# One core, a four-layer transformer kernel: the tail of expert routing in another form

## The chip, the cores and the metric

The kernel runs on one core of a Trainium2 chip, as one program. The metric is the device time of one execution in microseconds (us), the median of several. Engines are TensorE (PE in the rows), VectorE (DVE), ScalarE (ACT), GpSimd (POOL), and SyncE (SP), which issues most DMA transfers.

## The reference

Eight batches of 100 tokens of width 512 pass through four residual layers: an alignment with a context of 722 rows by dynamic time warping, a mixture of 16 experts of which each token takes 3, latent attention, and a second mixture. The change touches the second layer, on its side that decides which expert gets which token:

```
raw_gate = softmax(einsum('btd,de->bte', x, gate))          # 8 x 100 x 16
_, topk_idx = top_k(raw_gate, 3)
mask = one_hot(topk_idx, 16).sum(axis=2)
gate_topk = mask * raw_gate
gate_topk = gate_topk / maximum(sum(abs(gate_topk), -1), 1e-12)
hidden = relu(einsum('btd,edh->bteh', x, W1) + b1)
out = einsum('bte,bted->btd', gate_topk, einsum('bteh,ehd->bted', hidden, W2) + b2)
```

Here x is already the layer-normalised output of the first layer.

## The kernel before

The program is a row of stages, `distances`, `warp`, `route`, `experts`, `attend_full`, `attend`, `feed_forward`. Each is a block with one instruction stream for each engine. A stage frees its semaphores and passes a barrier of all engines before the next begins. Inside a stage the order on an engine is the order of the code, and semaphores are the only ties between engines. `link` (a helper) makes each VectorE instruction wait for the one before.

`route` has two parts. In **the path stream**, for each batch b, TensorE multiplies the path with the context rows (`along_path`, L1025), VectorE adds the product to x (L1101), widens the next path and takes layer norm statistics (L1105 to L1110), TensorE transposes the result (`turn`, L1033), VectorE copies that to SBUF (`keep_T`, L1097), and TensorE makes the 16 logits of each token (`logits`, L1041), all in one PSUM tile `pl`. SP meanwhile stores x and the normalised rows to DRAM.

In **the tail** everything is done for all 8 batches at once. VectorE takes the softmax (with an exponential on ScalarE), `max` and `max_index` per batch, one-hot masks `hot`, their sum `chosen` (L1134), and the gates. TensorE counts ranks with two f32 products (L1056, L1057). VectorE adds totals over batches one by one, counts the tiles of 128 slots that each expert needs, and gets the slot of every (token, choice) pair. Slots are then inverted into tables by slot: VectorE compares each slot with 35 tile starts (`over`, L1163) and makes `in_tile` (the place inside a tile, 24 x 128 elements, L1169), GpSimd makes `of_tile` with three channels (1, token, gate; L1002 to L1006), and 24 f32 products on TensorE sum `in_tile` against `of_tile` (L1065). VectorE reads off the indices `gidx`, `oidx` and the gates `gate_s` (L1172 to L1175), and GpSimd gathers the first three tiles of rows (L1012). The loop `keep_awake` (L81) fills TensorE with f32 products of the identity whose results nobody reads: 36 before the inversion, 40 after it. Each f32 product is two rows (passes) in the trace.

`experts` starts with two transposes of gathered tiles (L1257). Then it runs 27 tiles of 128 slots, each with 32 + 8 f32 products; the third gathered tile is first used in the middle of the first of them.

Of the kernel before, what the change touches and what calls it, by code (L numbers as in the profile page):

```python
# [15 lines left out]
P = 128  # L16
# [20 lines left out]
NG = 3  # L37
# [863 lines left out]
def route(nc, io, res):  # L901

    ctx = ExitStack()
    with ctx:
# [9 lines left out]
        logit = sb("logit", [S, B, E_N])  # L914
        prob = sb("prob", [S, B, E_N])
        lmax, lsum = sb("lmax", [S, B]), sb("lsum", [S, B])
        top = sb("top", [S, B, 8])
        topi = sb("topi", [S, B, 8], U32)
        topf = sb("topf", [S, B, 8])
        tsum = sb("tsum", [S, B])  # L920
        iota_e = sb("iota_e", [S, E_N])
        hot = [sb(f"hot{k}", [S, B, E_N]) for k in range(TOPK)]
        chosen = sb("chosen", [S, B, E_N])
        before = sb("before", [S, S])
        tot = sb("tot", [S, B, E_N])
        off = sb("off", [S, B + 1, E_N])
        ntile, tiles_to, one_e = sb("ntile", [S, E_N]), sb("tiles_to", [S, E_N]), sb("one_e", [S, E_N])
        slot = sb("slot", [S, B, E_N])
        picked = sb("picked", [S, B, E_N])
        slotf = sb("slotf", [S, TOPK, B])  # L930

        KB, NT = TOPK * B, SLOT_TILES
        in_tile = res["reach_mem"][0:S, 0:KB * P].rearrange("p (i j) -> p i j", j=P)
        spare = ctx_rows[0:S, :, :].rearrange("p t d -> p (t d)")
        over = spare[:, 0:KB * (NT + 1)].rearrange("p (i t) -> p i t", t=NT + 1)
        of_tile = spare[:, KB * (NT + 1):KB * (4 * NT + 1)].rearrange("p (i c t) -> p i c t", c=3, t=NT)
        tile0, slot0, token = sb("tile0", [S, NT + 1]), sb("slot0", [S, P]), sb("token", [S, TOPK, B])
        tnum, within, dump = sb("tnum", [S, KB]), sb("within", [S, KB]), sb("dump", [P, 2])
        where_to = sb("where_to", [P, NT])
        ptab = pb("ptab", [P, 3 * NT])  # L940
        over_ok, tile_ok, of_ok, in_ok, tab_mm, idx_ok, kept_rows = (sem(n) for n in (
            "over_ok", "tile_ok", "of_ok", "in_ok", "tab_mm", "idx_ok", "kept_rows"))
# [3 lines left out]
        pl = pb("pl", [S, B, E_N])  # L946
        prank = pb("prank", [S, B * E_N])
        ptot = pb("ptot", [S, B, E_N])
        path_in, gate_in = res["path_in"], sem("gate_in")
        pathf_ok, px_ok, x_ok, var_ok, st_ok, xn_ok = (sem(n) for n in ("pathf_ok", "px_ok", "x_ok", "var_c", "st_c", "xn_ok"))  # L950
        pt_ok, xnT_ok, pl_ok, sub_ok, exp_ok, cs_ok = (sem(n) for n in ("pt_ok", "xnT_ok", "pl_ok", "sub_ok", "exp_ok", "cs_ok"))
        cs0, hot_ok, rank_ok = (sem(n) for n in ("cs0", "hot_ok", "rank_ok"))
# [27 lines left out]
        def _(pool):  # L980
            pool.iota(iota_e[:, :], pattern=[[1, E_N]], base=0, channel_multiplier=0,
                      allow_small_or_imprecise_dtypes=True).then_inc(cs_ok, 1)
            pool.memset(before[:, :], 1.0).then_inc(cs0, 1)
            pool.wait_ge(cs0, 1)

            pool.affine_select(out=before[:, :], in_=before[:, :], compare_op=ALU.is_gt, fill=0.0, base=0,
                               pattern=[[1, S]], channel_multiplier=-1).then_inc(cs_ok, 1)
            pool.iota(tile0[:, :], pattern=[[P, NT + 1]], base=0, channel_multiplier=0,
# [3 lines left out]
            pool.iota(token[:, :, :], pattern=[[0, TOPK], [S, B]], base=0, channel_multiplier=1,  # L992
                      allow_small_or_imprecise_dtypes=True).then_inc(cs_ok, 1)
            pool.iota(dump[:, 0:1], pattern=[[0, 1]], base=XT, channel_multiplier=1,
                      allow_small_or_imprecise_dtypes=True).then_inc(cs_ok, 1)
            pool.iota(dump[:, 1:2], pattern=[[0, 1]], base=-XT, channel_multiplier=-1,
# [3 lines left out]
            pool.wait_ge(cs_ok, 8)  # L1000
            pool.wait_ge(over_ok, 1)
            pool.tensor_tensor(of_tile[:, :, 0, :], over[:, :, 0:NT], over[:, :, 1:NT + 1], ALU.subtract).then_inc(tile_ok, 1)  # L1002
            pool.wait_ge(tile_ok, 1)
            pool.tensor_tensor(of_tile[:, :, 1, :], of_tile[:, :, 0, :],
                               token[:, :, :].rearrange("p k b -> p (k b)").unsqueeze(2).broadcast_to([S, KB, NT]), ALU.mult).then_inc(of_ok, 1)
            pool.tensor_tensor(of_tile[:, :, 2, :], of_tile[:, :, 0, :],  # L1006
                               res["gates"][:, :, :].rearrange("p k b -> p (k b)").unsqueeze(2).broadcast_to([S, KB, NT]), ALU.mult).then_inc(of_ok, 1)

            pool.wait_ge(idx_ok, 1)
            pool.wait_ge(kept_rows, 32 * B)  # L1010
            for i in range(NG):
# [1539 lines left out]
```

## Time and profile before

| what | value |
|---|---|
| median of 3 runs | 1208.29 us (1207.68 to 1208.56) |
| the profiled execution, its own time | 1209.34 us |
| its span, first to last instruction | 1207.7 us |
| mean granted TensorE clock | 0.95 of full |
| TensorE busy | 1074.1 us (89%) |
| VectorE busy | 460.0 us (38%) |
| ScalarE busy | 336.7 us (28%) |
| GpSimd busy | 224.6 us (19%) |

The share of an engine is an average over the stages; what a change in `route` is worth is read inside that stage. `route` runs from 274.7 us to about 379 us of the span, `experts` from there to about 800 us. Starts in the rows are us from the start of the span.

### The profile page before, as it was taken

The numbers are of one execution on the slowest core, as the hardware profiler recorded it, in microseconds if no ns is written. First come the engines' busy times: TensorE is split into PE (matmuls) and PEld (weight loads), VectorE is DVE, ScalarE is ACT, GpSimd is POOL, SyncE is SP. The second block draws the span as 40 slices with busy tenths as digits, with TensorE's granted clock in tenths as the row PEclk, the third lists the DMA queues.
The fourth block names the chain that finished last, engine by engine and source line by source line (L and its number), as shares of the span: only waits on it lengthen the run. The fifth ranks groups of instructions, "written<-read, shape, count | busy, mean of one in ns | idle before, by whom it ended". The sixth has DMA issues, their size and how long they took to land. (4 is left out here: it accounts for less than half of the span.)

```text
span 1207.7 us, 17529 instructions
## 1 busy us (share of the span) xinstructions
PE 1074.1 (89%) x5498; PEld 702.9 (58%) x5499; DVE 460.0 (38%) x1698; ACT 336.7 (28%) x802; POOL 224.6 (19%) x341
## 2 busy tenths in 40 slices
PE   8966679937949999999999999949999999999997
PEld 8952235524448777677766777635446665555554
DVE  7847888883570000000000010036765463121212
ACT  4424756770001222222222222214245430000000
POOL 0963021110021121121111111210030001121211
PEclk9978799968969999999999999969999999999999
DMA  8876005128404575856596555560021005000000
GB/s 302 227 169 219 1 1 183 53 99 220 152 14 164 156 246 183 283 193 218 182 311 201 182 182 183 173 196 10 0 77 64 1 1 157 1 1 1 14 14 28
DMA packets 71763, 152.84 MB, mean 127 GB/s; under 512 B 12026, under 2 KB 16258, under 8 KB 70870
## 3 DMA queue, kind: packets, MB, share of 16 engines
q1 hardware_dynamic: 63454, 131.21, 32.0%
q0 software_dynamic: 6928, 17.04, 6.3%
q10 hardware_dynamic: 1320, 3.84, 1.2%
q8 instruction: 30, 0.49, 0.2%
q14 instruction: 31, 0.25, 0.1%
HBM read 131.83 MB, written 20.25 MB: 126 GB/s over the span
## 5 line engine op out<-in xcount | busy, mean ns | idle before, releaser
L1305 ACT ACTIVATE att<-phid,b 128x128 f32<-128x128 f32 x216 | 79.3, 367 | 306.8 <-PE phid L1274 306.8
L1327 DVE TENSOR_TENSOR att<-py,att 128x512 f32<-128x512 f32 x27 | 18.7, 692 | 367.3 <-PE py L1282 367.3
L1274 PEld LDWEIGHTS phid<-tiles,shared 128*128 128x128 f32 x896 | 111.5, 192 | 37.4 <-issue 37.4
L1274 PEld LDWEIGHTS phid<-tiles,Wmem 128*128 128x128 f32 x832 | 103.5, 192 | 39.1 <-issue 39.1
L1274 PE MATMUL phid<-tiles,shared 128*128 x896 | 114.4, 276 | 1.2 <-issue 0.5
L1274 PE MATMUL phid<-tiles,Wmem 128*128 x832 | 106.3, 276 | 5.8 <-issue 4.5
L1282 PE MATMUL py<-shared,att 128*128 128x512 f32 x224 | 110.0, 593 | 0.0
L1282 PE MATMUL py<-Wmem,att 128*128 128x512 f32 x208 | 102.3, 594 | 0.4 <-DMA att<-in_b 0.4
L2365 PE MATMUL acc<-tiles 128*128 128x400 f32 x256 | 90.6, 505 | 0.0
L2431 DVE SCALAR_TENSOR_TENSOR tiles<-bf,shared 128x400 f32<-128x400 f32 x64 | 32.4, 567 | 130.3 <-PE bf L2350 129.6
L2324 PE MATMUL bf<-shared,Wmem 128*128 128x400 f32 x192 | 70.0, 501 | 2.0 <-PEq L49 1.3
L2365 PEld LDWEIGHTS acc<-tiles 128*128 128x128 f32 x256 | 47.1, 190 | 40.4 <-issue 8.6
L1349 POOL DMA_INDIRECT sum_d<-att,to_row x27 | 43.0, 1594 | 144.4 <-DVE att L1330 144.4
L2274 POOL TENSOR_TENSOR tiles<-tiles 128x400 f32<-128x400 f32 x32 | 32.4, 1033 | 153.8 <-DVE tiles L2431 153.8
L2324 PEld LDWEIGHTS bf<-shared,Wmem 128*128 128x128 f32 x192 | 36.1, 190 | 29.9 <-issue 2.0
L887 DVE TENSOR_TENSOR_SCAN cost_mem<-reach_mem,cost_mem,enter 128x93 bf16<-128x93 bf16 x115 | 47.2, 411 | 11.8
L1770 DVE RECIPROCAL shared<-shared 128x400 f32<-128x400 f32 x16 | 42.4, 2652 | 21.0 <-ACT shared L1677 20.7
L2291 ACT COPY outT<-acc 128x400 f32<-128x400 f32 x4 | 1.8, 495 | 172.4 <-PE acc L2365 172.4
L81 PE MATMUL px<-ident 128*128 128x128 f32 x188 | 27.2, 317 | 24.0 <-DMA path<-ctx_rows 16.3
L1492 PE MATMUL ba<-shared,Wmem 128*128 128x400 f32 x128 | 46.1, 504 | 2.6 <-DVE qT L1773 1.5
L1282 PEld LDWEIGHTS py<-shared,att 128*128 128x128 f32 x224 | 36.1, 192 | 13.4 <-issue 13.4
L209 POOL TENSOR_SCALAR Wmem<-slots_row,pos_k 128x128 bf16<-128x128 f32 x48 | 39.9, 850 | 20.6 <-DVE pos_k L143 20.6
(388 smaller groups left out, 1715.5 us busy)
## 6 DMA issues: line engine op xcount, KB each, us to landing
Wmem<-in_W SPq DMA_DIRECT2D x16, 2048.0 KB, 14.2
shared<-in_W SPq DMA_DIRECT2D x16, 2048.0 KB, 11.9
cT<-in_ctxT SPq DMA_DIRECT2D x8, 1444.0 KB, 11.8
ctx_rows<-in_ctx SPq DMA_DIRECT2D x8, 1280.0 KB
Wmem<-in_Wkv SPq DMA_DIRECT2D x2, 2048.0 KB, 9.2
att<-in_b SPq DMA_DIRECT2D x16, 256.0 KB, 14.3
tiles<-in_WoT SPq DMA_DIRECT2D x4, 1024.0 KB
Wmem<-in_WiT SPq DMA_DIRECT2D x3, 1024.0 KB, 7.1
```

Source lines behind the costliest of these rows:

```text
L209: pool.tensor_scalar(sel[:, b, t, :], slots_row[:, :], pos[:, t, b:b + 1], None, ALU.is_equal)
L887: dve.tensor_tensor_scan(walk[:, q, 1:NO], code[:, q, :], enter[:, :], walk[:, q, 0:1], ALU.mult, ALU.max).then_inc(scanned_r, 1)
L1274: ins = pe.matmul(ph[j % NH][:, :], W1[u][:, k, j * P:(j + 1) * P], xgT[:, bass.ds(w, 1), k * P:(k + 1) * P].rearrange("p o t -> p (o t)") ...
L1282: ins = pe.matmul(py[:, :], hT[:, j - 2, :], W2[u][:, j - 2, :], start=j == 2, stop=j == HJ + 1)
L1305: act.activation(hT[:, j, :], ph[j % NH][:, :], ACT.Relu, bias=b1[:, bass.ds((e + u) * HJ + j, 1)]).then_inc(relu_ok, 1)
L1349: pool.indirect_dma_start(out=res["sum_d"], out_offset=bass.IndirectOffsetOnAxis(ap=to_row[:, 0:1], axis=0), in_=y[:, :], in_offset=None, ...
L1492: ins = pe.matmul(qk_b[j % 3][:, 0:NH2], w, lnT[:, k, g * NH2:(g + 1) * NH2], start=k == 0, stop=k == KD - 1)
L1770: link(dve.reciprocal(inv[j % 2][:, :], inv[j % 2][:, :]))
L2274: pool.tensor_tensor(hs[i % 4][:, :], h1[i % 4][:, :], h2[i % 2][:, :], ALU.add).then_inc(hs_ok, 1)
L2324: pe.matmul(bank[i % NBK][:, 0:NT4], Wi[k][:, f * P:(f + 1) * P], xT[:, k, g * NT4:(g + 1) * NT4], start=k == 0, stop=False)
L2365: ins = pe.matmul(acc[k][:, 0:NT4], WoT[:, f, k * P:(k + 1) * P], hs[i % 4][:, :], start=f == 0, stop=f == FJ - 1)
L2431: dve.scalar_tensor_tensor((h1[i % 4], h2[i % 2])[k][:, :], bank[i % NBK][:, 0:NT4], 0.0, wb[k][:, g * NT4:(g + 1) * NT4], ALU.max, ALU.mu ...
```

## The change

It rewrites the tail and moves part of it:

- **Three best per batch, in the stream.** `best(b)` takes `max` and `max_index` straight from the PSUM logits (two banks in turn, so TensorE now waits on `pl_rd`), makes `hot` for the three choices and `chosen`, in bf16. `below_best(b)` subtracts the largest logit. Both are done for batch b-2 in iteration b; the last two batches follow after the last `keep_T`. No softmax is needed to choose.
- **Ranks.** A scan along batches (`upto`) replaces the additions per batch; three bf16 products give totals and ranks. Tiles of an expert come from one comparison, one reduction and one scan.
- **Slots inverted by codes.** The tile number is the slot as an integer, shifted right by 7. `same` (24 x 34) marks the tile, `of_tile` has two bf16 channels (batch code by VectorE, row code by ScalarE), `in_tile` is bf16, and 24 bf16 products yield one code from which both indices are made. GpSimd does nothing in between.
- **Gates last.** Softmax sums and gates come after the indices, split into three bf16 parts, and have 24 bf16 products of their own.
- **Gathers.** Two in `route`, the third at the head of GpSimd's part of `experts`.
- **`keep_awake`.** 8 before the last `turn`, 7 after the logits, 10 after the ranks, 10 after the indices' products and 16 after the gates' products, in place of 36 and 40.

The core of the diff:

```diff
+            def best(b):
+                dve.wait_ge(pl_ok, b + 1)
+                link(dve.max(top[:, b, :], pl[b % 2]))
+                dve.max_index(topi[:, b, :], top[:, b, :], pl[b % 2]).then_inc(pl_rd, 1)
+                dve.wait_ge(pl_rd, 2 * b + 1)
+                link(dve.tensor_tensor(hot[:, :, b, :], iota_e[...], topi[:, b, 0:TOPK][...], ALU.is_equal))
+                link(dve.tensor_tensor(chosen[:, :, b], hot[:, 0, b, :], hot[:, 1, b, :], ALU.add))
+                link(dve.tensor_tensor(chosen[:, :, b], chosen[:, :, b], hot[:, 2, b, :], ALU.add))
+            def below_best(b):
+                dve.tensor_scalar(logit[:, b, 0:E_N], pl[b % 2], top[:, b, 0:1], None, ALU.subtract).then_inc(pl_rd, 1)
...
                 if b:
                     keep_T(b - 1)
+                if b >= 2:
+                    best(b - 2)
+                    below_best(b - 2)
             keep_T(B - 1)
-            dve.wait_ge(pl_ok, B)
-            link(dve.tensor_reduce(lmax[:, :], pl[:, :, :], AX, ALU.max))
...
+            best(B - 2)
+            below_best(B - 2)
+            best(B - 1)
+            dve.tensor_tensor_scan(upto[...], fresh[...], chosen[...], 0.0, ALU.mult, ALU.add).then_inc(hot_ok, 1)
+            below_best(B - 1)
...
+            link(dve.tensor_copy(sloti[:, :], slotf[:, :]))
+            link(dve.tensor_scalar(tnum[:, :], sloti[:, :], 7, None, ALU.logical_shift_right))
+            dve.scalar_tensor_tensor(within[:, :], tnum[:, :], -float(P), slotf[:, :], ALU.mult, ALU.add)
+            dve.tensor_tensor(same, tile0[...], tnum[...], ALU.is_equal).then_inc(same_ok, 1)
+            dve.wait_ge(same_ok, 1)
+            dve.tensor_tensor(of_tile[:, :, 0, :], same, batch1[...], ALU.mult).then_inc(batch_ok, 1)
...
@@ TensorE
+                if n == B:
+                    pe.wait_ge(x_ok, B - 1)
+                    keep_awake(pe, px_whole[0], ident, 8)
...
-            keep_awake(pe, px_whole[0], ident, 36)
-            pe.wait_ge(of_ok, 2)
+            keep_awake(pe, px_whole[1], ident, 10)
+            pe.wait_ge(batch_ok, 1)
+            pe.wait_ge(row_ok, 1)
...
             ins.then_inc(tab_mm, 1)
-            keep_awake(pe, px_whole[0], ident, 40)
+            keep_awake(pe, px_whole[1], ident, 10)
+            for i in range(KB):
+                if i % B == 0:
+                    pe.wait_ge(gate_ok, i // B + 1)
+                ins = pe.matmul(pgate, in_tile[:, i, :], of_gate[:, i, :, :]..., start=i == 0, stop=i == KB - 1)
+            ins.then_inc(gate_mm, 1)
+            keep_awake(pe, px_whole[1], ident, 16)
```

**VectorE, end of the path stream, before.** From the normalisation of the last batch (`cost_mem<-x_res`) on; `xg_sb` holds the transposed rows, `pl` the logits.

```order
L1110 TENSOR_SCALAR cost_mem<-x_res,mv_c,rstd_c 100x512
L1097 COPY xg_sb<-pt 128x400 x2
L1115 TENSOR_REDUCE lmax<-pl 100x8
L1116 TENSOR_TENSOR logit<-pl,lmax 100x128
L1118 TENSOR_REDUCE lsum<-prob 100x8
```

The same place in the change:

```order
L1140 TENSOR_SCALAR cost_mem<-x_res,mv_c,rstd_c 100x512
L1113 COPY xg_sb<-pt 128x400
L1117 MAX top<-pl 100x8
L1118 MAX_INDEX topi<-top,pl 100x8
L1120 TENSOR_TENSOR hot<-iota_e,topi 100x3x16
L1122 TENSOR_TENSOR chosen<-hot 100x16
L1123 TENSOR_TENSOR chosen<-chosen,hot 100x16
L1126 TENSOR_SCALAR logit<-pl,top 100x16
L1113 COPY xg_sb<-pt 128x400
L1117 MAX top<-pl 100x8
```

The two copies of transposed rows stood side by side; now the six instructions for batch 5 stand between them, and those for batches 6 and 7 behind them.

**TensorE, from the last transposes to the end of `route`, before.** `px<-ident` is `keep_awake`.

```order
L1033 MATMUL pt<-ident,cost_mem 128x100 x4
L1041 MATMUL pl<-gate_w,xg_sb 100x16 x8
L1056 MATMUL prank<-chosen,before 100x128
L1057 MATMUL ptot<-chosen,ones 100x128
L81 MATMUL px<-ident 128x128 x36
L1065 MATMUL ptab<-ctx_rows,reach_mem 128x102 x24
L81 MATMUL px<-ident 128x128 x40
```

The same place in the change:

```order
L81 MATMUL px<-ident 128x128 x8
L1032 MATMUL pt<-ident,cost_mem 128x100 x4
L1042 MATMUL pl<-gate_w,xg_sb 100x16 x8
L81 MATMUL px<-ident 128x128 x7
L1062 MATMUL pt<-upto,all_rows 100x16
L1063 MATMUL prank<-chosen,before 100x128
L1064 MATMUL prank<-upto,all_rows 100x128
L81 MATMUL px<-ident 128x128 x10
L1071 MATMUL ptab<-ctx_rows,reach_mem 128x68 x24
L81 MATMUL px<-ident 128x128 x10
L1077 MATMUL px<-ctx_rows,reach_mem 128x102 x24
L81 MATMUL px<-ident 128x128 x16
```

Two long loops of fillers became five short ones, and a second set of 24 products, for the gates, stands behind the first.

## Rows read from the trace of the kernel before

**Rows 1.** Timeline of TensorE: start, length, instruction, count, [idle before, releaser].

```profile
332.10 0.80 PE L1041 MATMUL pl<-gate_w,xg_sb 128*100 128x16 f32 x8
...
343.87 0.75 PE L1056 MATMUL prank<-chosen,before 100*100 100x128 f32 x2 [5.58 <-DVE chosen L1134]
...
352.76 11.15 PE L81 MATMUL px<-ident 128*128 128x128 f32 x72 [7.71 <-DVE ctx_rows L1163]
363.75 5.50 PE L1065 MATMUL ptab<-ctx_rows,reach_mem 100*128 100x102 f32 x48
369.08 9.12 PE L81 MATMUL px<-ident 128*128 128x128 f32 x80
379.13 1.07 PE L1257 MATMUL ptx<-ident,xg_sb 128*128 128x128 f32 x8 [0.93 <-PEq L49]
...
389.33 0.60 PE L1257 MATMUL ptx<-ident,xg_sb 128*128 128x128 f32 x4
```

**Rows 2.** Stretches: us, busy (count) by engine, granted clock, DMA share, GB/s.

```profile
331.80:335.00 3.20, 1.25 (x14) 1.16 (x13) 2.63 (x7) 1.17 (x2) 0.00 (x0) 0.98 0.00 0
335.00:338.30 3.30, 3.29 (x20) 3.18 (x20) 0.85 (x2) 0.32 (x1) 0.00 (x0) 0.50 0.41 124
338.30:352.70 14.40, 1.17 (x4) 0.83 (x4) 12.21 (x72) 0.31 (x1) 0.00 (x0) 0.50 0.00 1
352.70:358.80 6.10, 6.04 (x28) 6.07 (x29) 6.03 (x5) 0.00 (x0) 5.95 (x3) 0.50 0.00 1
...
369.20:378.20 9.00, 9.00 (x81) 8.81 (x79) 0.71 (x4) 0.00 (x0) 3.02 (x3) 1.00 0.28 87
378.20:381.60 3.40, 1.11 (x10) 0.90 (x9) 1.42 (x2) 1.38 (x3) 0.00 (x0) 1.00 0.29 60
```

**Rows 3.** Timeline of VectorE, end of the path stream.

```profile
331.96 0.69 DVE L1101 TENSOR_TENSOR x_res<-x_res,px 100x512 f32<-100x512 f32 x1 [2.88 <-PE px L1025]
...
334.71 0.57 DVE L1097 COPY xg_sb<-pt 128x400 f32<-128x400 f32 x1
335.80 0.58 DVE L1097 COPY xg_sb<-pt 128x400 f32<-128x400 f32 x1 [0.52 <-PE pt L1033]
```

**Rows 4.** Timeline of VectorE, the tail.

```profile
340.20 0.71 DVE L1122 MAX8 top<-prob 100x8 f32<-100x16 f32 x8
...
341.03 0.17 DVE L1125 FIND_INDEX8 topi<-top,prob 100x8 uint32<-100x16 f32 x1
...
343.53 0.29 DVE L1134 TENSOR_TENSOR chosen<-chosen,hot 100x128 f32<-100x128 f32 x1
...
343.94 0.17 DVE L1138 TENSOR_SCALAR tsum<-tsum 100x8 f32<-100x8 f32 x1
...
351.58 1.03 DVE L1163 TENSOR_TENSOR ctx_rows<-slotf,tile 100x840 f32<-100x840 f32 x1
...
354.39 6.22 DVE L1169 TENSOR_TENSOR reach_mem<-slot,within 100x1024 f32<-100x1024 f32 x3
```

**Rows 5.** One line, L1169: count, ns min/median/max, first and last start.

```profile
L1169 DVE TENSOR_TENSOR reach_mem<-slot,within x3: 1224/2579/2579, 354.4 to 358.0; 100x1024 f32<-100x1024 f32 x3
```

**Rows 6.** Timeline of GpSimd, the tail.

```profile
357.00 2.54 POOL L1006 TENSOR_TENSOR ctx_rows<-ctx_rows,gates 100x816 f32<-100x816 f32 x1
370.32 1.11 POOL L1012 DMA_INDIRECT xg_sb<-xn_d,gidx  x1 [10.79 <-DVE gate_s L1175]
```

**Rows 7.** Groups of the page, the scan of `warp`: busy us, mean ns, idle before.

```profile
L887 DVE TENSOR_TENSOR_SCAN cost_mem<-reach_mem,cost_mem,enter 128x93 bf16<-128x93 bf16 x115 | 47.2, 411 | 11.8
```

**Rows 8.** Timeline of TensorE, bf16 products of `warp`.

```profile
85.58 0.80 PE L538 MATMUL pfil<-Wmem,onesw 128*128 128x128 bf16 x6
86.18 0.34 PE L536 MATMUL pidx<-where,Wmem 128*128 128x2 bf16 x6
86.39 0.80 PE L538 MATMUL pfil<-Wmem,onesw 128*128 128x128 bf16 x6
```

**Rows 9.** One line of ScalarE, L514: ns min/median/max.

```profile
L514 ACT ACTIVATE reach_mem<-rank_w,one x11: 772/829/836, 101.1 to 180.2; 128x460 bf16<-128x460 bf16 x10, 128x414 bf16<-128x414 bf16 x1
```

**Rows 10.** One line, L1343, the gathers in `experts`, issue to landing.

```profile
DMA to landing us min/median/max: 3.3/4.5/6.4
```

More of the change, by code:

```diff
@@ L923, in route @@
[L923 to L930, printed above, removed]
-        KB, NT = TOPK * B, SLOT_TILES
-        in_tile = res["reach_mem"][0:S, 0:KB * P].rearrange("p (i j) -> p i j", j=P)
@@ L934, in route @@
[L934 to L940, printed above, removed]
@@ new lines, in route @@
+        hot = sb("hot", [S, TOPK, B, E_N], BF16)
+        chosen, upto, fresh = (sb(n, [S, E_N, B], BF16) for n in ("chosen", "upto", "fresh"))
+        before, all_rows = sb("before", [S, S], BF16), sb("all_rows", [S, S], BF16)
+        limits, beyond = sb("limits", [S, MORE_TILES]), sb("beyond", [S, E_N, MORE_TILES])
+        ntile, tiles_to, one_e = sb("ntile", [S, E_N]), sb("tiles_to", [S, E_N + 1]), sb("one_e", [S, E_N])
+        slot, picked = sb("slot", [S, B, E_N]), sb("picked", [S, TOPK, B * E_N])
@@ new lines, in route @@
+        KB, NT = TOPK * B, SLOT_TILES
+        slotf = sb("slotf", [S, KB])
+        sloti, tnum = sb("sloti", [S, KB], I32), sb("tnum", [S, KB], I32)
+        within = sb("within", [S, KB], BF16)
+        in_tile = res["reach_mem"][0:S, 0:KB * P // 2].bitcast(BF16).rearrange("p (i j) -> p i j", j=P)
+        spare = ctx_rows[0:S, :, :].rearrange("p t d -> p (t d)")[:, 0:3 * KB * NT].bitcast(BF16)
+        same = spare[:, 0:KB * NT].rearrange("p (i t) -> p i t", t=NT)
+        of_tile = spare[:, KB * NT:3 * KB * NT].rearrange("p (i c t) -> p i c t", c=2, t=NT)
@@ new lines, in route @@
+        of_gate = spare[:, 3 * KB * NT:6 * KB * NT].rearrange("p (i c t) -> p i c t", c=3, t=NT)
+        tile0, slot0 = sb("tile0", [S, NT], BF16), sb("slot0", [S, P], BF16)
+        batch1, row1, dump = sb("batch1", [S, KB], BF16), sb("row1", [S, 1]), sb("dump", [P, 1])
+        gpart = sb("gpart", [S, KB, 3], BF16)
+        grest = sb("grest", [S, KB])
+        code, where_to = sb("code", [P, NT]), sb("where_to", [P, NT])
+        ptab = pb("ptab", [P, 2 * NT])
+        same_ok, batch_ok, row_ok, in_ok, gate_ok, tab_mm, gate_mm, idx_ok, kept_rows, pl_rd = (sem(n) for n in (
+            "same_ok", "batch_ok", "row_ok", "in_ok", "gate_ok", "tab_mm", "gate_mm", "idx_ok", "kept_rows", "pl_rd"))
@@ L1077, in _ @@
             act.activation(prob[:, :, :], logit[:, :, :], ACT.Exp).then_inc(exp_ok, 1)
+            act.wait_ge(cs_ok, NCONST)
+            act.wait_ge(same_ok, 1)
+            act.activation(of_tile[:, :, 1, :], same, ACT.Copy, scale=row1[:, 0:1]).then_inc(row_ok, 1)
         @block.vector
@@ L1170, in _ @@
                                   within[:, k * B:(k + 1) * B].unsqueeze(2).broadcast_to([S, B, P]), ALU.is_equal).then_inc(in_ok, 1)
+            dve.tensor_copy(res["table"][:, 0:E_N + 1], tiles_to[:, :])
             dve.wait_ge(tab_mm, 1)
-            dve.tensor_copy(res["gidx"][:, 0:NT], ptab[:, NT:2 * NT])
-            link(dve.tensor_scalar(where_to[:, :], ptab[:, 0:NT], dump[:, 1:2], dump[:, 0:1], ALU.mult, ALU.add))
-            dve.tensor_tensor(res["oidx"][:, 0:NT], where_to[:, :], ptab[:, NT:2 * NT], ALU.add)
@@ L1178 @@
+            for k in range(TOPK):
+                n = slice(k * B, (k + 1) * B)
+                dve.tensor_tensor(of_gate[:, n, :, :], same[:, n, :].unsqueeze(2).broadcast_to([S, B, 3, NT]),
+                                  gpart[:, n, :].unsqueeze(3).broadcast_to([S, B, 3, NT]), ALU.mult).then_inc(gate_ok, 1)
+            dve.wait_ge(gate_mm, 1)
+            dve.tensor_reduce(res["gate_s"][:, 0:NT], pgate.rearrange("p (c t) -> p t c", t=NT), AX, ALU.add)
 INNER, HEADS, DH = 512, 8, 64
```

159 lines of the change are left out of this document (74 added, 85 removed).

## The prediction

> **What bounds the kernel now.** I read the stage boundaries first, on TensorE's timeline. The path stream ends with the logits of batch 7 (338.30), the first product of `experts` starts at 379.13 [rows 1, 2], and in the 41 us between TensorE does nothing that anyone reads except two short rank products and the 48 passes of L1065. So `route`'s tail is a pure latency chain, and every us cut from it moves the whole rest of the program forward: `experts` starts with a barrier, and its loads of the second expert's weights are issued behind that barrier too, so they move along. Second I asked who holds the chain at each point:
>
> - 338.30 to 352.70: VectorE. Busy 12.21 of 14.40 us with 72 instructions, most with about 0.17 us of fixed cost [rows 2, 4].
> - 352.76 to 363.75: TensorE's own 72 filler passes, at half clock for the first 6 us, 28 rows in 6.10 us, 0.218 us each [rows 1, 2]. VectorE's `in_tile` ends at 360.61, GpSimd's last channel at 359.54 [rows 4, 6]; the fillers last longer and hold the 48 passes back by 3.1 us.
> - 369.08 to 378.20: 80 more filler passes at full clock, 81 rows in 9.00 us, 0.111 us each. Indices are ready and the gathers begin at 370.32 [rows 1, 2, 6]; nothing but these fillers holds the barrier, and TensorE's next product stands 0.93 us behind them [rows 1].
>
> The end of `route` is therefore set by TensorE's last filler, and I follow the chain to that point in both kernels.
>
> **The change, step by step.** Unit prices: 128 elements on VectorE 0.29 us, 840 elements 1.03 us [rows 4], so 0.16 us plus 1.04 ns per element; an instruction of 8 to 24 elements 0.17 to 0.20; a gap of 0.035 us between linked instructions.
>
> 1. *Stream.* `best` is MAX8 (0.16 alone; eight side by side took 0.71), the index search (0.17 and its load, 0.25 together), 48 elements (0.21), twice 16 elements (0.34), and `below_best` 0.17: with five gaps 1.3 us per batch [rows 4]. VectorE idles 2.88 us per batch waiting for L1025 [rows 3], and TensorE needs its result only after the next six long products. So batches 0 to 4 cost nothing. If that cover were gone it would be 1.3 us for each of 5 batches. Batch 5's six instructions stand ahead of the last `keep_T`: that copy started at 335.80, and now starts at 335.28 + 1.3 = 336.6 and ends at 337.2 [rows 3]. Logits of batch 7 are then 0.80 us, if the clock is full [rows 1], to 338.0. VectorE's work for batch 6 ends at 338.5, batch 7's at 339.65. The scan over 128 elements is unseen at that size; 93 took 0.41 [rows 7], so between 0.41 and 0.57, and I take 0.55. `chosen` and `upto` are there at **340.2**; before it was 343.82 [rows 4].
> 2. *Ranks.* TensorE has 7 fillers (14 passes) to finish first: 338.0 + 14 x 0.111 = 339.6 at full clock, + 14 x 0.218 = 341.1 at half. The first rows show the clock at half from 335.0 after only about 2 us of idling between the last context product and the last transposes [rows 2]; now 8 fillers stand there, but TensorE idles again from about 335.9 to 337.2. I take the low clock, hence 341.1, and 0.25 for the totals: **341.35**.
> 3. *Slots.* 96 elements twice (0.52), a scan of 16 (0.19), 128 elements (0.29), 384 twice (1.12), three of 24 (0.54), `same` 816 (1.01), nine gaps (0.33): 4.0 us, to **345.35**. Before, the same stretch ran from 345.1 to 352.6, over three times as many instructions.
> 4. *Inversion.* VectorE: one batch channel 1.05, `in_tile` 3 x 1.22, to **350.1**. The 1.22 is the fastest of the three before; the other two took 2.58 each while GpSimd's multiplications ran beside them [rows 5, 6], and GpSimd is silent now. ScalarE's channel: 460 elements took 0.83 [rows 9], so 816 take at most 1.47, done at 346.9, before the first third of `in_tile` (347.6). The last 8 of 24 bf16 products: twelve took 0.81 [rows 8], so 0.55, and 0.15 to land: **350.8**. Before it was 369.25.
> 5. *Indices and gates.* Reduction and `gidx` 0.5 (the two gathers follow, 2.5 us, covered), `where_to` and `oidx` 0.45, eleven small gate instructions with gaps 2.55, `of_gate` 3 x 1.03: 357.4. Ten fillers (2.2 to 4.4 us) lie in TensorE's wait for it. Last 8 products 0.7: **358.1**. All of this is new behind the index table: before, the gates cost 0.7 us ahead of it plus one GpSimd channel.
> 6. *Last fillers.* 16, so 32 passes x 0.111 = 3.55 at full clock, to **361.65**.
>
> Sum: 378.20 - 361.65 = 16.5 us. By parts: fillers at the end, 9.1 down to 3.55, give 5.6; the gate chain takes 7.3 back; the rest, 18.2, is the chain to the index table (369.25 to 350.8, less rounding). The extra constants on GpSimd lie in front of the stream, where VectorE waits anyway.
>
> The third gather now goes out behind the barrier, at about 0.5 to 1 us into `experts`, and is issued in 1.1 us. It is used 10.2 us after the stage's first product (389.33 against 379.13) [rows 1], and gathers there land in 3.3 to 6.4 us amid the weight loads [rows 10]: covered by about 2 us; if not, at most a few us once.
>
> *A rule weighed.* The bf16 operands could make the wide VectorE comparisons faster than the f32 rows. All rows of two-operand instructions of this width are f32 [rows 4, 5], so the trace does not show bf16: at an unchanged rate 1.22 us, at double rate 0.16 + 0.53 = 0.69 us. I take the f32 row. The Trainium skill, "VectorE: DVE Perf Modes" (the perf-mode tier table), says that a `tensor_tensor` on bf16 in SBUF runs at twice the f32 rate. "Vector Engine (DVE) Microarchitecture Reference" (Performance modes) adds that an operand which repeats one element ran at the single rate; that is the layout of `in_tile`, `of_tile` and `of_gate`. No run here shows either yet.
>
> **Rivals.**
>
> - *Forecast, 0.60:* as summed. The profiled execution would be 1209.34 - 16.5 = 1192.8; the median shown lies 1.05 us under the profiled time, so 1208.3 - 16.5 = 1191.8; I say **1192**. Its own range is 1190 to 1194, for the sizes of unseen instructions (about 1 us each way) and the 7 fillers (0.9).
> - *Low clock at the end, 0.22:* between the rank products and the index products VectorE keeps TensorE waiting over 5 us, of which 10 fillers cover 2.2 to 4.4, and the gate products come in three bursts. For it: about 2 us of idling sufficed before [rows 2]. Against it: the clock came back after 6.1 us of dense passes, even at half clock [rows 2], and index products plus 10 fillers are about that long. The last 32 passes then take 7.0 instead of 3.55: 1195.3. If `experts` also starts low, its first products pay up to 3 us more: 1198.
> - *Double rate, 0.08:* one `of_tile` channel saves 0.42, `in_tile` 3 x 0.53, `of_gate` 3 x 0.42: 3.3 us, 1188.7.
> - *Third gather late, 0.05:* it queues behind 4 MB of weights that SP issues in the same us and lands after them, some 3 to 4 us after its use: 1195.5.
> - *Slower, 0.02:* VectorE's added work in the stream doesn't fit. Its result feeds back to TensorE over `pl_rd`, in lock step. The cover is 2.88 us per batch; to lose the 16.5 us over six iterations it must overrun by 2.75 each, so cost 5.6 us instead of 1.3, 0.9 us per instruction. An instruction of 24 elements did take 0.67 beside GpSimd's work, but GpSimd has none in the stream. At 1.1 us each, it would be 1208.3 - 16.5 + 6 x 3.7 = 1214.
> - *Nothing gained, 0.03:* a wait that I don't see at the stage's end, such as for the gathers or stores, keeps the barrier near 378. Against it: gathers begin at 370.32 before and the stores were out long ago.
>
> **Numbers.** 1192. The range reaches from the double rate to the low clock at the end with part of a cold start: 1188.5 to 1197.5; less than 2 in 10 lies outside. What a measurement of this kernel can tell from no change is 0.2%, 2.4 us. Faster 0.95, same 0.02, slower 0.03 (part of the last two).
>
> **What would show it.** In the profile of the change: `upto` written near 340; `same` near 345.5; three L1174 instructions of 1.2 us each with nothing on GpSimd beside them; the first gather near 351.5; the last filler near 361.7 and the first product of `experts` 0.93 behind; `experts` and all later stages as long as before. L1131 must keep its 6.2 us rhythm. I would be wrong if that rhythm stretches, if the last 32 fillers last 7 us, if L1174 takes 0.7, or if TensorE waits for L1363's gather in the first tile.

## The result and the profile after

| | before | after |
|---|---|---|
| median of 4 runs, us | 1207.99 (1207.40 to 1208.56) | 1192.56 (1192.04 to 1194.04) |
| the profiled execution, own time | 1209.34 | 1192.04 |
| its span | 1207.7 | 1190.4 |
| mean granted TensorE clock | 0.950 | 0.958 |

The ratio after / before is 0.9874 [0.9857, 0.9891]: 15.4 us less.

Busy times of the profiled execution after, first page:

```profile
PE 1064.0 (89%) x5447; PEld 694.0 (58%) x5448; DVE 464.1 (39%) x1711; ACT 338.1 (28%) x803; POOL 218.8 (18%) x342
```

TensorE has 10 us less of busy time than before and VectorE 4 us more. These sums say nothing of the order of the work; the tail's timeline does. TensorE after, in the columns of [rows 1]:

```profile
336.75 3.33 PE L81 MATMUL px<-ident 128*128 128x128 f32 x14
339.88 0.22 PE L1062 MATMUL pt<-upto,all_rows 100*100 100x16 bf16 x1
...
340.18 3.66 PE L81 MATMUL px<-ident 128*128 128x128 f32 x20
...
348.57 0.63 PE L1071 MATMUL ptab<-ctx_rows,reach_mem 100*128 100x68 bf16 x8 [0.50 <-DVE reach_mem L1174]
349.01 4.34 PE L81 MATMUL px<-ident 128*128 128x128 f32 x20
...
355.53 0.55 PE L1077 MATMUL px<-ctx_rows,reach_mem 100*128 100x102 bf16 x8 [0.37 <-DVE ctx_rows L1200]
355.92 3.80 PE L81 MATMUL px<-ident 128*128 128x128 f32 x32
360.66 1.06 PE L1285 MATMUL ptx<-ident,xg_sb 128*128 128x128 f32 x8 [0.94 <-PEq L49]
363.16 4.56 PE L1302 MATMUL phid<-tiles,Wmem 128*128 x24 [1.44 <-ACT att L1326]
367.55 1.02 PE L1310 MATMUL py<-Wmem,att 128*128 128x512 f32 x2
```

The first product of `experts` starts at 360.66 where it started at 379.13 [rows 1]. That is 18.5 us, but not all of it is the change's: the tail itself began earlier in this trace. VectorE after:

```profile
324.06 0.69 DVE L1131 TENSOR_TENSOR x_res<-x_res,px 100x512 f32<-100x512 f32 x1 [1.15 <-PE px L1024]
...
330.27 0.69 DVE L1131 TENSOR_TENSOR x_res<-x_res,px 100x512 f32<-100x512 f32 x1 [1.47 <-PE px L1024]
...
338.22 0.42 DVE L1150 TENSOR_TENSOR_SCAN upto<-fresh,chosen 100x128 bf16<-100x128 bf16 x1
340.14 0.26 DVE L1156 TENSOR_TENSOR beyond<-pt,limits 100x96 f32<-100x96 f32 x1 [1.27 <-PE pt L1062]
...
343.06 1.00 DVE L1169 TENSOR_TENSOR ctx_rows<-tile,tnum 100x816 bf16<-100x816 bf16 x1
...
345.02 3.49 DVE L1174 TENSOR_TENSOR reach_mem<-slot,within 100x1024 bf16<-100x1024 bf16 x3
...
349.50 0.18 DVE L1180 TENSOR_SCALAR gidx<-code 128x34 int32<-128x34 f32 x1
...
352.63 2.85 DVE L1200 TENSOR_TENSOR ctx_rows<-ctx_rows,gpart 100x816 bf16<-100x816 bf16 x3
```

The last addition to x starts at 330.27, against 331.96 before [rows 3]. Over all traces of this study that start lies between 329.8 and 334.3 us, and the two at the ends of that range are kernels with the same code ahead of it. So I measure from it. I call "tail" the time from the last addition to x to the first product of `experts` (L1257 before, L1285 after), and "first tile" the time from there to its first `py` product.

- Tail: 47.17 before (331.96 to 379.13), 30.39 after (330.27 to 360.66): 16.78 less.
- First tile: 5.74 before, 6.89 after: 1.15 given back.
- From there to the end of the span: 822.8 in both.

Together 15.63 less; the medians differ by 15.4.

### The profile page after: what moved, and what is told of

Read it like the earlier page. It is cut to its first block and busy times, and to the rows that moved or that the text cites. A ratio compares the mean times of both kernels' runs of the same rounds, so it can differ in the third digit from the quotient of the medians.

```text
span 1190.4 us, 17449 instructions
## 1 busy us (share of the span) xinstructions
PE 1064.0 (89%) x5447; PEld 694.0 (58%) x5448; DVE 464.1 (39%) x1711; ACT 338.1 (28%) x803; POOL 218.8 (18%) x342
## 5 line engine op out<-in xcount | busy, mean ns | idle before, releaser
L1024 PE MATMUL px<-ctx_rows,cost_mem 128*100 128x512 f32 (+1 forms) x96 | 42.7, 595 | 0.0
## 6 DMA issues: line engine op xcount, KB each, us to landing
shared<-in_W SPq DMA_DIRECT2D x16, 2048.0 KB, 12.1
```

Source lines behind the costliest of these rows:

```text
L1024: ins = pe.matmul(px[b % 2][:, :], pathf[0:r, b % NPF * CT + t, :], ctx_rows[0:r, b * CT + t, :], start=t == 0, stop=t == CT - 1)
```

## The experiments

Each kernel was timed beside the kernel before; the ratio is to that. The two columns before the last are from its one profiled execution, measured as above. The kernels from "after, again" to "best three after the stream" ran on one chip, the next four on another and the last four on a third. Each ratio is to the kernel before on the same chip, so kernels of two chips are compared by their ratios.

| kernel | median us (runs) | ratio [95%] | tail | first tile | sum against before |
|---|---|---|---|---|---|
| before | 1207.99 (4) | | 47.17 | 5.74 | |
| after, again | 1194.11 (6) | 0.9868 [0.9847, 0.9888] | 30.46 | 6.82 | -15.6 |
| no last 16 fillers | 1190.91 (5) | 0.9842 [0.9823, 0.9860] | 25.74 | 7.22 | -20.0 |
| no gate chain | 1188.29 (5) | 0.9835 [0.9815, 0.9855] | 26.01 | 5.37 | -21.5 |
| best three after the stream | 1201.30 (6) | 0.9929 [0.9910, 0.9947] | 37.51 | 6.86 | -8.5 |
| before, 16 + 16 fillers | 1205.62 (12) | 0.9968 [0.9958, 0.9979] | 41.67 | 8.20 | -3.0 |
| after, f32 products | 1203.24 (6) | 0.9948 [0.9935, 0.9962] | 40.07 | 5.60 | -7.2 |
| after, GpSimd beside | 1196.16 (4) | 0.9885 [0.9867, 0.9903] | 35.54 | 5.25 | -12.1 |
| after, 3 gathers in route | 1193.87 (4) | 0.9881 [0.9862, 0.9900] | 29.83 | 5.39 | -17.7 |
| gates first, no last 16 | 1194.58 (6) | 0.9874 [0.9855, 0.9894] | 30.49 | 8.20 | -14.2 |
| no tail fillers | 1190.09 (5) | 0.9842 [0.9824, 0.9861] | 26.44 | 7.33 | -19.1 |
| 3 and 3 fillers | 1188.76 (5) | 0.9831 [0.9813, 0.9848] | 26.20 | 7.55 | -19.2 |
| before, 16 + 16, 2 gathers | 1205.95 (11) | 0.9966 [0.9952, 0.9980] | 40.39 | 7.56 | -5.0 |

The sum of one trace follows the ratio times 1208.3 us within 2 us for all but one kernel (3 gathers, where the ratio says -14.4).

**The changed kernel again, unedited.**

> The changed kernel again, as the base line for what runs beside it: 1192.0 to 1193.5 us. In its first profile the last filler ended at 359.72 us, the first product of experts stood at 360.66, and the first tile's first 24 products ran partly at half clock (4.56 us in place of 2.94 before). If that low stretch belongs to the kernel, it shows again at the same place; if it is chance, it is gone or elsewhere.

Tail and first tile came out at 30.46 and 6.82, within 0.1 us of the first trace.

**No last 16 fillers.**

```diff
-            keep_awake(pe, px_whole[1], ident, 16)
```

> The changed kernel without the last 16 fillers. Theory: they alone hold the end of route once the gates are read; VectorE's last instruction ended at 356.39 and TensorE's last filler at 359.72, so route ends 3.2 us earlier: 1189.3 us. Rival: the fillers pay for themselves, since without them TensorE idles over the barrier and the whole first tile of experts begins at half clock; then 2 to 3 us are given back and the time is 1191.5 to 1192.5.

TensorE's last filler of the logits' loop and the start of `experts`:

```profile
339.30 1.81 PE L81 MATMUL px<-ident 128*128 128x128 f32 x14
...
358.98 1.94 PE L1284 MATMUL ptx<-ident,xg_sb 128*128 128x128 f32 x8 [1.25 <-PEq L49]
```

The median fell by 3.2 us. The trace shows 4.7 less in the tail, of which some 1.3 is something else: the 14 passes after the logits took 1.81 us here, at full clock, and 3.33 in the kernel after. The first tile paid 0.4 us for its colder start. So these fillers cost about 3 us and bring 0.4. The intervals of the two ratios just overlap; the wait for the fillers in the trace is what shows the cost.

**No gate chain.** VectorE's eleven gate instructions and three `of_gate`, the 24 gate products and the 10 fillers ahead of them are gone, so every gate is the same constant; the 16 fillers stay.

```diff
-            link(dve.tensor_reduce(lsum[:, :], prob[:, :, 0:E_N], AX, ALU.add))
...
-            dve.tensor_reduce(res["gate_s"][:, 0:NT], pgate.rearrange("p (c t) -> p t c", t=NT), AX, ALU.add)
+            dve.memset(res["gate_s"][:, 0:NT], 0.333)
```

> The changed kernel without the gate chain: no softmax sums, no gate parts, no second set of 24 products and not the 10 fillers before them; all gates are a constant, 0.333. Theory: the gate chain is on the path that sets the end of route. The 16 last fillers then follow the index products at 349.0 and end at about 354.6 to 356.0 in place of 359.72, by the clock: 3.7 to 5.1 us less, 1187.5 to 1189. Rival: the gathers or the barrier hold the stage anyway (gathers were issued by 352.3 and land some 3 us later); then at most 1 to 2 us less, 1191.

TensorE, and GpSimd's last gather:

```profile
349.45 5.45 PE L81 MATMUL px<-ident 128*128 128x128 f32 x32
356.51 1.06 PE L1260 MATMUL ptx<-ident,xg_sb 128*128 128x128 f32 x8 [1.62 <-PEq L49]
```

```profile
351.83 0.95 POOL L1011 DMA_INDIRECT xg_sb<-xn_d,gidx  x1 [0.30 <-issue]
```

The last filler ended 5 us earlier, measured from the last addition to x, but the tail lost only 4.4 us: TensorE waits 1.62 us behind its last filler where it waited 0.94. The last gather was issued at 351.83 here. Its landing, not a filler, released the stage (below, at "gates first").

**Best three after the stream.** The softmax-free choice stays, but all its instructions come after the last `keep_T`, and the logits of all batches stay in PSUM, so TensorE never waits on `pl_rd`.

```diff
-                if b >= 2:
-                    best(b - 2)
-                    below_best(b - 2)
...
+            dve.wait_ge(pl_ok, B)
+            for b in range(B - 1):
+                best(b)
+                below_best(b)
```

> The changed kernel with all eight batches' three best taken after the last copy, none in the stream; the logits of all batches are kept in two PSUM banks. Theory: in the stream this work was free. Behind it, seven batches at 1.5 us and the last at 1.25 follow the logits; the last copy starts 1.2 us earlier. The rank products stand at about 348.5 in place of 339.88: plus 8.6 us, 1201 us, and the rhythm of 6.2 us per batch in the stream is unchanged. Rival: the work in the stream costs there too (TensorE's wait on the logits' banks, a VectorE that comes late); then the stream is shorter here and the loss under 6 us, 1198 or less.

VectorE, the end of its stream and its scan:

```profile
331.78 0.69 DVE L1130 TENSOR_TENSOR x_res<-x_res,px 100x512 f32<-100x512 f32 x1 [2.89 <-PE px L1025]
...
336.83 0.18 DVE L1116 MAX8 top<-pl 100x8 f32<-100x16 f32 x1 [0.97 <-PE pl L1041]
...
348.00 0.42 DVE L1148 TENSOR_TENSOR_SCAN upto<-fresh,chosen 100x128 bf16<-100x128 bf16 x1
```

VectorE's idle time before an addition to x is 2.89 here, 2.88 before [rows 3] and 1.47 in the kernel after; the additions are 6.20 and 6.21 us apart all the same. So `best`, 1.42 us a batch, was paid wholly out of idle time. Outside the stream it costs 7.1 us of tail and 7.2 of median, where 8.6 was expected: `upto` is ready 8.3 us later, but VectorE then no longer waits 1.27 us for the 7 fillers.

**Before, with 16 + 16 fillers instead of 36 + 40.**

```diff
-            keep_awake(pe, px_whole[0], ident, 36)
+            keep_awake(pe, px_whole[0], ident, 16)
...
-            keep_awake(pe, px_whole[0], ident, 40)
+            keep_awake(pe, px_whole[0], ident, 16)
```

> The kernel before with its fillers alone changed: 36 to 16 ahead of the inversion and 40 to 16 behind it. Theory: these fillers held 3 to 4 us in the middle (they ended at 363.9, the operands were there at 360.6) and all but 0.9 us of the end. Gain 3 to 4 + 24 x 2 x 0.111 = 5.3: 8.5 to 9.5 us, 1198.5 to 1199.5 us, so more than half of what the change as a whole gives. Rival: the fillers are needed, with fewer of them the clock is at half in the 48 passes and in the first tile of experts, which gives 3 us or more back: 1202 or more.

TensorE:

```profile
350.74 6.50 PE L81 MATMUL px<-ident 128*128 128x128 f32 x32 [7.71 <-DVE ctx_rows L1163]
357.58 5.60 PE L1065 MATMUL ptab<-ctx_rows,reach_mem 100*128 100x102 f32 x48 [0.33 <-POOL ctx_rows L1006]
363.02 3.76 PE L81 MATMUL px<-ident 128*128 128x128 f32 x32
371.60 1.94 PE L1257 MATMUL ptx<-ident,xg_sb 128*128 128x128 f32 x8 [4.83 <-PEq L49]
```

GpSimd's last gather, and its line's landing time:

```profile
366.93 0.94 POOL L1012 DMA_INDIRECT xg_sb<-xn_d,gidx  x1 [0.30 <-issue]
```

```profile
DMA to landing us min/median/max: 3.5/3.5/3.6
```

The stretch behind the new stage's start, in the columns of [rows 2]:

```profile
371.60:376.00 4.40, 3.42 (x15) 3.02 (x16) 1.42 (x2) 1.38 (x3) 0.00 (x0) 0.50 0.69 127
```

SP's first load of the new stage, which needs nothing of the gathers, starts at the same time:

```profile
371.57 0.35 SPq L1228 DMA_DIRECT2D b<-in_b1T  x1
```

The fillers end at 366.78, yet the stage ends 4.8 us later. The last gather lands at 366.93 + 3.5 = 370.4, and 1.1 us after that the next stage begins, on SP too: it is the stage's end that waits, not TensorE for its tile. The first tile then runs at half clock (0.50, against 1.00 in [rows 2]) and takes 2.5 us more. The tail lost 5.5 us. Cutting 44 fillers out of the kernel before thus gave 3.6 us by medians and not the 8.5 that fillers alone would have: some 3 us went to the landing, 2.5 to the clock. In the middle the cut did all that was expected: the index products end 33.25 us after the last addition to x, 4.0 us earlier than before.

**The same, with the third gather behind the stage's end.**

```diff
-            for i in range(NG):
+            for i in range(2):
...
+            pool.indirect_dma_start(out=xg[:, 2, :], out_offset=None, in_=res["xn_d"],
```

> The kernel before with 16 and 16 fillers, as in e_before_fill16 (1205.6 us), and its third gather moved behind the barrier. Theory: the landing of the last gather is what held the barrier 4.8 us beyond the last filler there; one gather less lets it go 1.26 us earlier, 3.5 us beyond the filler: 1204.3. Rival: something else holds the barrier, and TensorE still waits 4.8 us: 1205.6.

TensorE, and GpSimd's last gather:

```profile
374.30 1.87 PE L1257 MATMUL ptx<-ident,xg_sb 128*128 128x128 f32 x8 [3.54 <-PEq L49]
```

```profile
369.65 0.95 POOL L1012 DMA_INDIRECT xg_sb<-xn_d,gidx  x1 [0.30 <-issue]
```

TensorE's wait at the stage's end fell from 4.83 to 3.54 us, one gather issue (1.25 us), as the landing of the last gather says. The ratios can't tell the two kernels apart.

**Gates first.** On the kernel without the last 16 fillers, VectorE's gate instructions stand ahead of its wait for the index table.

```diff
+            dve.wait_ge(exp_ok, 1)
...
+                                   gpart[:, n, :].unsqueeze(3).broadcast_to([S, B, 3, NT]), ALU.mult).then_inc(gate_ok, 1)
             dve.wait_ge(tab_mm, 1)
             link(dve.tensor_reduce(code[:, :], ptab[:, :]..., AX, ALU.add))
```

> The changed kernel without the last 16 fillers and with VectorE's gate chain moved ahead of the reading of the indices; otherwise the same instructions. To be compared with e_last0 (1190.9 us; first product of experts 28.2 us after the last addition to x is due). Theory: the stage's barrier waits until the last gather has landed, about 1.4 + 3.6 us after the indices plus 1.1 of barrier. Indices come 5 us later here, so this becomes the last to end: the first product of experts comes 1.5 to 2 us later than in e_last0, and 6 us after the indices: 1192.7. Rival: the gathers do not hold the barrier, and only the sum of VectorE's work counts: then the time is that of e_last0 or 0.6 better, 1190.3 to 1191.

TensorE, and GpSimd's last gather:

```profile
352.69 1.54 PE L1077 MATMUL px<-ctx_rows,reach_mem 100*128 100x102 bf16 x24
360.27 1.94 PE L1284 MATMUL ptx<-ident,xg_sb 128*128 128x128 f32 x8 [6.05 <-PEq L49]
```

```profile
355.69 0.95 POOL L1011 DMA_INDIRECT xg_sb<-xn_d,gidx  x1 [0.30 <-issue]
```

The work is the same, but the last gather goes out 25.9 us after the last addition to x, against 21.1 in the kernel after and 19.8 in "no last 16 fillers"; it lands at about 359.1, and the stage ends at 360.3. The tail is 4.75 us longer than in "no last 16 fillers" and the time 3.9 us by the ratios, measured on two chips. I had expected 1.5 to 2, on a wrong base: I took that kernel's tail to be 28.2 us, and it measured 25.74. About 1.5 us of the 4.75 are the 14 passes after the logits, at half clock here (3.33 us) and at full clock there (1.81), and the first tile took 1 us more. What the order costs is therefore some 3 us of tail; the 6 us expected from the indices to the first product were 6.3. Four kernels now fit one sum: issue of the last gather + 3.5 us + 1.1 us. It gives 351.83 + 4.6 = 356.4 for "no gate chain" (seen 356.51), 371.5 for 16 + 16 (371.60), 374.2 with two gathers (374.30), 360.3 here (360.27). For the kernel after it gives 351.39 + 4.6 = 356.0, and the fillers end later (the stage starts at 360.66).

**F32 products.** Masks, codes and gate parts stay as they are, but `same`, `of_tile`, `of_gate` and `in_tile` are f32.

```diff
-        in_tile = res["reach_mem"][0:S, 0:KB * P // 2].bitcast(BF16).rearrange("p (i j) -> p i j", j=P)
+        in_tile = res["reach_mem"][0:S, 0:KB * P].rearrange("p (i j) -> p i j", j=P)
```

> The changed kernel with the wide tables same, of_tile, of_gate and in_tile in f32, so that both sets of 24 products are f32 again, two passes each (TensorE; ScalarE and VectorE write 4 bytes per element). Theory: bf16 saves on TensorE only. VectorE's instructions keep their length (1.16 and 1.00 us), the last 8 index products take 16 x 0.2 = 3 us at half clock in place of 0.63, the last 8 gate products 1.8 in place of 0.55: plus 3.5 us, 1196. Rival: VectorE gains from bf16 as well, then its wide instructions are longer too, by over 0.2 us each, and the loss is 5 us or more.

TensorE, and then VectorE's `in_tile` line (ns, least, median, most):

```profile
346.23 9.75 PE L1071 MATMUL ptab<-ctx_rows,reach_mem 100*128 100x68 f32 x48 [3.66 <-DVE reach_mem L1174]
...
360.47 5.70 PE L1077 MATMUL px<-ctx_rows,reach_mem 100*128 100x102 f32 x48
```

```profile
L1174 DVE TENSOR_TENSOR reach_mem<-slot,within x3: 1217/1217/1219, 344.9 to 347.1; 100x1024 f32<-100x1024 bf16 x3
```

I expected 3.5 us; it was 9.7 in the tail and 9 by the ratios. In bf16, 16 of the 24 products are done while VectorE still makes the next third of `in_tile`, and only eight follow it. In f32 there are 48 passes at half clock, 0.20 us each, and they no longer keep up: they end 7.6 us behind `in_tile` in place of 0.7, so the index table is read 6.4 us later. The 48 f32 passes for the gates add the other 3.3 us, nearly all at full clock (0.12 us each). VectorE doesn't notice: 1217 ns either way.

**GpSimd beside.** Two f32 multiplications of 100x816 on GpSimd, whose results go nowhere, beside `in_tile`.

```diff
+            pool.wait_ge(batch_ok, 1)
...
+            for n in range(2):
+                pool.tensor_tensor(other[:, 2 + n, :], other[:, 0, :], other[:, 1, :], ALU.mult)
```

> The changed kernel with two f32 multiplications of 100x816 on GpSimd, both inputs in SBUF, started when in_tile starts; nobody uses their result. Theory: GpSimd's work beside in_tile was what made two of its three instructions 2.58 us before; so at least two of the three become 2.2 to 2.6 us here against 1.16, and index table and end of route come 2 to 3 us later: 1195. Rival: those instructions were slow before for being f32, and GpSimd does not matter; then they stay at 1.2 and the time at 1192.5.

GpSimd, and VectorE's `in_tile` line:

```profile
349.32 5.66 POOL L1011 TENSOR_TENSOR ctx_rows<-ctx_rows 100x816 f32<-100x816 f32 x2 [70.15 <-DVE ctx_rows L1176]
```

```profile
L1178 DVE TENSOR_TENSOR reach_mem<-slot,within x3: 1220/2922/2932, 349.1 to 353.1; 100x1024 bf16<-100x1024 bf16 x3
```

The pattern of [rows 5] is back: the first third at 1.22 us, the others at 2.9. The index table came 3.5 us later and the last fillers met part of a low clock (5.43 us instead of 3.80), so the tail grew by 5.1; the shorter first tile left 3.5 in the sum. By the ratios it is 1.3 to 2.1 us against the kernel after and 0.5 against "3 gathers in route", which ran on the same chip, and the intervals overlap. So the longer instructions and the later index table are shown, a longer time of the whole kernel is not.

**Third gather back in `route`.**

```diff
-            for i in range(2):
+            for i in range(3):
```

> The changed kernel with the third gather put back into route, behind the other two. Theory: it is hidden in either place; GpSimd would issue it from 352.7 to 353.6, 6 us before the last filler ends, and in experts it is used 11.3 us after the stage starts: no change, 1192.5 within 0.5. Rival: behind the barrier it competes with the weight loads or holds something back; then this kernel is 1 us or more faster.

```profile
360.27 1.06 PE L1285 MATMUL ptx<-ident,xg_sb 128*128 128x128 f32 x8 [0.94 <-PEq L49]
```

Nothing moves: 0.94 us behind the last filler, as in the kernel after. The median of 1193.87 lies above the 1192.5 within 0.5 that was expected, but the ratio (0.9881) can't be told from that of the kernel after. The index table is early enough for three gathers.

**No fillers in the tail at all.**

```diff
-                    keep_awake(pe, px_whole[0], ident, 8)
-            keep_awake(pe, px_whole[1], ident, 7)
-            keep_awake(pe, px_whole[1], ident, 10)
-            keep_awake(pe, px_whole[1], ident, 10)
-            keep_awake(pe, px_whole[1], ident, 16)
```

> The changed kernel without any of the 51 fillers in and around the tail (8, 7, 10, 10 and 16). Theory: the chain is VectorE's and needs TensorE's clock little: the route tail is no longer than in e_last0, within 0.5 us, since without 7 fillers the ranks come up to 1.2 us earlier and products at half clock cost 0.2 to 0.5 at each of three places; but experts starts at half clock and its first tile takes 1.5 to 3 us more than at full. Together 1190 to 1192. Rival: with a cold TensorE the transposes and logits, the two sets of 24 products and the first tile each lose over 1 us: 1194 or more.

```profile
353.11 2.70 PE L1073 MATMUL px<-ctx_rows,reach_mem 100*128 100x102 bf16 x24 [4.49 <-DVE ctx_rows L1195]
357.05 1.94 PE L1280 MATMUL ptx<-ident,xg_sb 128*128 128x128 f32 x8 [1.24 <-PEq L49]
```

All 51 fillers together cost 3 to 4 us (ratios 0.9868 and 0.9874 against 0.9842): 4 us of tail, less what they buy, a first tile of 6.8 to 6.9 us in place of 7.3. The ratio is that of "no last 16 fillers", so no cost of the other 35 is shown.

**Three and three.** 7 fillers to 3 after the logits, 16 to 3 at the end; the other loops stay.

```diff
-            keep_awake(pe, px_whole[1], ident, 7)
+            keep_awake(pe, px_whole[1], ident, 3)
...
-            keep_awake(pe, px_whole[1], ident, 16)
+            keep_awake(pe, px_whole[1], ident, 3)
```

> A version to beat the change: 3 fillers in place of 7 after the logits, 3 in place of 16 at the end. Theory: at half clock 7 fillers end 1.2 us after upto is ready (3 end in time), and 3 at the end lie beside VectorE's last reduction. The first product of experts comes 4 to 4.5 us earlier than in the changed kernel; the first tile costs at most 1.5 us more: 1189 to 1190. Rival: the clock is lost for longer and gives it back: 1192.

```profile
336.45 1.63 PE L81 MATMUL px<-ident 128*128 128x128 f32 x6
338.51 0.26 PE L1062 MATMUL pt<-upto,all_rows 100*100 100x16 bf16 x1 [0.43 <-DVE upto L1150]
...
356.42 1.80 PE L1285 MATMUL ptx<-ident,xg_sb 128*128 128x128 f32 x8 [0.94 <-PEq L49]
359.20 4.93 PE L1302 MATMUL phid<-tiles,Wmem 128*128 x24 [0.98 <-ACT att L1326]
```

The rank product now waits for VectorE (0.43) and not the other way round, and the stage ends 4.3 us earlier than after. At 0.9831 [0.9813, 0.9848] it has the lowest ratio of the kernels with the whole computation. Its interval just clears that of the kernel after (from 0.9857), though not that of the repeat on another chip (0.9847 to 0.9888), and it can't be told from the kernel with no tail fillers.

## Why the prediction was right, step by step

Times in us after the last addition to x starts:

| step | forecast | after |
|---|---|---|
| 1, `upto` there | 8.24 | 8.37 |
| 2, comparison of the totals starts | 9.39 | 9.87 |
| 3, `same` there | 13.39 | 13.79 |
| 4, `in_tile` ends | 18.14 | 18.24 |
| 4, index products end | 18.84 | 18.93 |
| 5, gate products end | 26.14 | 25.81 |
| 6, last filler ends | 29.69 | 29.45 |

- *Step 1, stream.* Held, and shown by "best three after the stream". `best` cost 1.42 us a batch where 1.3 was taken, the scan of 128 elements 0.42 where 0.55 was.
- *Step 2, ranks.* Held, 0.5 us late: the 7 fillers lasted 3.33 us and made VectorE wait 1.27. The logits ahead of them took 1.28 us, where full clock and 0.80 had been taken. The stretches after, the first at the fillers and the last two at the end, in the columns of [rows 2]:

```profile
335.00:338.30 3.30, 2.67 (x15) 2.70 (x16) 2.90 (x16) 0.00 (x0) 0.00 (x0) 0.63 0.20 71
338.30:341.00 2.70, 2.70 (x16) 2.69 (x15) 1.32 (x7) 0.33 (x1) 0.00 (x0) 0.50 0.00 0
...
356.00:359.00 3.00, 3.00 (x30) 3.00 (x29) 0.27 (x1) 0.00 (x0) 0.00 (x0) 1.00 0.00 0
362.00:365.00 3.00, 1.84 (x8) 1.85 (x9) 0.38 (x1) 0.70 (x2) 0.95 (x1) 0.69 0.70 187
```

  The choice of the low clock was a coin that fell right. In "no last 16 fillers" the same 14 passes ran at full clock.
- *Steps 3 and 4, slots and inversion.* Held: 3.92 us for 4.0, and 4.45 for 4.75, since the unlinked `in_tile` instructions overlap by 0.08 us each. `in_tile` took 1.22 us each, as the f32 row: the rival of the double rate is out. With f32 output it took 1217 ns and with bf16 1217 ns. The Trainium skill, "Vector Engine (DVE) Microarchitecture Reference" (Performance modes), says that an operand which repeats one element ran at the single rate. The trace agrees with it, 1217 ns. The general line of the Trainium skill, "VectorE: DVE Perf Modes" (the perf-mode tier table), would have given 0.69 and doesn't hold here. That the silence of GpSimd brings the index table forward is shown by "GpSimd beside": 1.22 us became 2.92, and the table came 3.5 us later. By the Trainium skill, "GPSIMD Engine Reference" (Specifications), GpSimd's way into SBUF is shared with VectorE and contended when a VectorE instruction has two SBUF inputs. The trace agrees with it; no run here tells this cause from another.
- *Step 4, products.* The duration was right (0.63 for the last eight). What bf16 is worth was not worked out in the prediction, and in the expectation of its experiment it was set far too low, 3.5 us for 9.7.
- *Step 5, gates last.* Right in length (6.9 us forecast 7.3). Its sense I had not seen. It looks like a detour of 7 us on the critical path, but the gathers' 5 us run beside it. Without it the tail is 4.4 us shorter, and with gates first it is longer by some 3 us.
- *Step 6, last fillers.* Right in length, full clock. But the sentence ahead of the sum, "nothing but these fillers holds the barrier", was wrong as a rule and right only by 1.3 us. GpSimd in the kernel before, the last gather of `route`, and its line's landing time:

```profile
373.00 0.95 POOL L1012 DMA_INDIRECT xg_sb<-xn_d,gidx  x1 [0.30 <-issue]
```

```profile
DMA to landing us min/median/max: 3.6/3.7/3.9
```

  That gather allowed the next stage at 373.0 + 3.7 + 1.1 = 377.8; the fillers' end made it 379.1 [rows 1]. The 5.6 us put down to the fillers at the end could be had only because the index table also came 18 us earlier. The kernel before with few fillers kept 3.6 of its 8.5. The rival "nothing gained" had named just such a wait, for the gathers; it exists, but moved forward with the index table and did not keep the stage near 378.
- *Low clock at the end.* The rival's condition failed for the 32 passes (clock 1.00, 3.80 us), but part of its price came in the next stage: granted clock 0.69 from 362 to 365, and the 24 `phid` passes took 4.56 us where the kernel before and "no gate chain" had 2.94. That is the 1.15 us given back in the first tile, and why 16.78 in the tail became 15.4 in the median. What decides whether the first tile starts low stays open: over the changed kernels it took 5.25 to 8.20 us with only loose relation to the fillers, and 16 of them at full clock did not prevent it.
- *Third gather late:* out, but closer than its cover said. Issued at 362.08 in the trace after, it landed 7.6 us later, beyond the 3.3 to 6.4 of [rows 10], and TensorE used its tile at 371.92, 2.2 us behind the landing. It made nobody wait, and moving it back changed nothing. Its line:

```profile
DMA to landing us min/median/max: 7.6/7.6/7.6
```

- *Slower, nothing gained:* out; the additions to x stayed 6.21 us apart.

That 1192 met 1192.56 so closely is in part luck: the logits and fillers came 0.5 us later than forecast, `in_tile` took 0.3 and the gate chain 0.4 us less, the first tile gave back 1.15 us that the sum did not hold, and the clock at the 7 fillers could have gone the other way.

Where the 15.4 us come from, then: the index table is ready 18.4 us earlier, and five things share in that. Choosing the three experts in the stream is worth 7 us. Having fewer fillers ahead of the inversion was worth 4.0 in the kernel before (36 to 16). The slot arithmetic takes 3.9 us where it took 7.5. The bf16 products are worth 6.4, in a stretch whose clock is at half. GpSimd's silence is worth 2.7 by [rows 5] and 3.5 in the experiment. Together these are more than 18.4, so they overlap, and no experiment separates them or tests the slot arithmetic alone. The shorter last loop adds its 5.6 because the gathers went out early enough. The gate chain takes 6.9 back, 5 of them beside the gathers, and the first tile 1.15.

## What to carry to other kernels

Ask of every stage's end not only which engine finishes last but when its last transfer lands: work that issues transfers goes ahead of work that doesn't, even if the chain on the engines gets no shorter. Small instructions go where their engine already idles in a loop, up to that idle time. Count filler products as work: in the two kernels they held the chain four times, and of the 4 us of tail that they cost in the second about 0.5 came back in the first tile.

## What the hardware showed that I had not expected

- The next stage starts 1.1 us after the last gather of GpSimd has landed, though no instruction of the stage waits for that landing; issue to landing is 3.4 to 3.9 us in `route` (once 5.2, in "3 gathers in route", where the fillers ended later still), and the sum fits four kernels within 0.1 us.
- An f32 product with 68 columns costs 0.20 us per pass at half clock, near the 0.218 of one with 128 columns [rows 2]: fewer columns save little there. In bf16 eight take 0.61 us.
- Two kernels with the same code ahead differ in whether a loop of fillers gets full or half clock (1.81 us for 14 passes in "no last 16 fillers", 3.33 in the kernel after), and the last addition to x starts up to 4.5 us apart. A difference of a few us read between the same instants of two traces needs an anchor.
